# Split fp16 products for the projections of batches 2 to 7 in a gated cross-attention and mixture kernel

## The reference

```
xn = layernorm(x)
q = Wq xn + bq;  k = Wk ctx + bk;  v = Wv ctx + bv        (256x256 weights, 512 columns per batch)
q, k = rotary(q), rotary(k);  16 heads of 16 channels
x  = x + tanh(g0) * (Wm softmax(q k / 4) v + bm)
x  = x + tanh(g1) * moe(layernorm(x))                     (8 experts, top 2, 512 -> 1024 -> 512)
```

## Time and profile before

| | |
|---|---|
| median of 3 runs | 1136.09 us (1134.47 to 1137.49) |
| profiled execution | 1133.16 us |
| its span | 1131.3 us |
| TensorE matmul, weight load | 1079.3, 443.7 us busy |
| VectorE, ScalarE, GpSimd | 801.2, 684.7, 378.6 us busy |
| phases 3 to 12 | some 32 us each |

### The profile page before, as it was taken

One profiled execution on the slowest core, in us unless ns is written; L12 is line 12 of the kernel. 1 busy time (PEld: TensorE's weight loads), 2 busy tenths in 40 slices (PEclk: granted clock), 3 DMA queues, 4 the chain that ended last, 5 costly groups with the idle time before them and its releaser, 6 DMA issues.

```text
span 1131.3 us, 19036 instructions
## 1 busy us (share of the span) xinstructions
PE 1079.3 (95%) x5988; PEld 443.7 (39%) x5988; DVE 801.2 (71%) x1595; ACT 684.7 (61%) x934; POOL 378.6 (33%) x489
## 2 busy tenths in 40 slices
PE   8998999999999999988989999999999999999997
PEld 3322333333333333332344444444444444444443
DVE  7878898898988887888377575756547565755632
ACT  1277777777777777788765574646446464653421
POOL 3673636848483865532220011110111101111101
PEclk9999999999999999999989999999999999999999
DMA  6336435323234323202258685758657476883433
GB/s 199 117 94 210 163 107 197 110 94 107 78 114 132 104 79 104 92 31 88 80 215 265 138 222 102 203 118 223 141 111 198 119 218 141 203 170 59 70 61 47
DMA packets 182671, 150.60 MB, mean 133 GB/s; under 512 B 122672, under 2 KB 144176, under 8 KB 182576
## 3 DMA queue, kind: packets, MB, share of 16 engines
q1 hardware_dynamic: 171680, 128.91, 40.3%
q0 software_dynamic: 7456, 17.57, 7.9%
q10 hardware_dynamic: 3440, 2.94, 1.0%
HBM read 73.80 MB, written 41.23 MB: 102 GB/s over the span
## 4 chain that ended last, share of the span: by engine, by line
PE 77%; DVE 9%; ACT 7%; issue 4%; DMA 2%; SPq 1%; POOL 0%; POOLq 0%; DVEq 0%; ACTq 0%
PE psum L1291 36%; PE psum L1292 10%; PE psum L364 7%; PE psum L351 6%; PE psum L240 6%; ACT W L545 5%; DVE MX L737 4%; PE psum L339 3%; PE psum L289 3%; PE psum L256 2%; PE psum L381 2%; PE psum L271 1%; ACT W L495 1%; PE psum L308 1%; PE psum L277 1%
## 5 line engine op out<-in xcount | busy, mean ns | idle before, releaser
L545 ACT ACTIVATE W<-psum,es 128x512 f32<-128x512 f32 x512 | 321.4, 688 | 72.9 <-PE psum L351 71.6
L737 DVE TENSOR_REDUCE MX<-psum 128x2 f32<-128x1024 f32 x256 | 310.4, 1219 | 50.0 <-PE psum L339 47.6
L1291 PE MATMUL psum<-W,xT 128*128 128x512 f16 x1248 | 273.7, 379 | 0.0
L1291 PEld LDWEIGHTS psum<-W,xT 128*128 128x128 f16 x1248 | 121.5, 98 | 148.5 <-issue 2.9
L351 PE MATMUL psum<-stg 50*128 50x512 f16 x512 | 142.9, 386 | 21.6 <-ACT W L545 16.4
L1564 POOL DMA_INDIRECT out<-yb,target x34 | 53.1, 1562 | 291.5 <-ACT yb L1393 289.0
L1496 DVE TENSOR_TENSOR hh<-sg,psum 128x512 f32<-128x512 f32 x68 | 46.4, 685 | 145.0 <-ACT sg L1380 145.0
L1291 PE MATMUL psum<-W,hT 128*128 128x512 f16 x648 | 144.3, 379 | 0.0
L364 PE MATMUL psum<-W 128*32 128x512 f32 x1024 | 136.4, 605 | 0.0
L1380 ACT ACTIVATE sg<-psum,i 128x512 f32<-128x512 f32 x68 | 46.3, 681 | 143.3 <-PE psum L1291 120.6
L620 DVE SCALAR_TENSOR_TENSOR W<-stg,scw,W 128x1024 f16<-128x1024 f32 x96 | 117.3, 1279 | 11.7 <-ACT W L613 11.7
(11 more groups left out here) (241 smaller groups left out, 1359.3 us busy)
## 6 DMA issues: line engine op xcount, KB each, us to landing
stg<-in_w SPq DMA_DIRECT2D x16, 2048.0 KB, 8.9
stg<-in_wo SPq DMA_DIRECT2D x8, 2048.0 KB, 10.3
stg<-scr SPq DMA_DIRECT2D x183, 64.0 KB, 2.3
Xs<-zero SPq DMA_DIRECT2D x40, 264.0 KB, 3.2
scr<-W SPq DMA_DIRECT2D x32, 256.0 KB, 3.1
W<-W SPq DMA_DIRECT2D x60, 128.0 KB, 2.1
xs<-in_x SPq DMA_DIRECT2D x8, 512.0 KB, 4.3
out<-xs SPq DMA_DIRECT2D x8, 512.0 KB, 3.1
```

The costliest lines, as they stand in the source:

```text
L545: act.activation(m.Pb[:, c % 2, hh, :], m.psT[tile % 2], ACT.Exp, scale=m.es[:, hb // 2:hb // 2 + 1]).then_inc(S["exped"], 1)
L737: dve.tensor_reduce(m.MX[:, hb % 2, c0:c0 + 9:8], m.psS[tile % 2], AX_X, ALU.max, negate=True).then_inc(S["maxed"], 1)
L1291: return pe.matmul(out, rows, m.wh[(e % 2, w)][:, wp, cols], start=start, stop=stop)
```

## The change

For batches 2 to 7 the q, k and v projections use fp16 halves. A number a is scaled by a power of two and split in an upper half, fp16(a), and a lower half, fp16(a - upper). A product is upper*upper + upper*lower + lower*upper: three fp16 matmuls for one fp32 matmul. A q or k job has 6 matmuls of 512 columns, a v job 12 of 256. Batches 0 and 1 stay fp32.

- Weights: their largest values (one new reduction of Wv on VectorE in phase -1, one all-partition maximum on GpSimd at the end of phase -1), six small scale operations on VectorE (phase 0, slot 3), three upper halves on ScalarE (phase 0, slot 5), three lower halves on VectorE (phase 0, slots 8, 10, 12).
- Context of batch b: five more small operations in `k_scale` (odd phase, slot 4), the upper half on ScalarE (`ctx_upper`, odd phase, slot 6), the lower half on VectorE (`ctx_lower`, odd phase, slot 8).
- Rows: `norm` gets a factor 2^10 by one more small operation on GpSimd, the upper half is a copy on ScalarE (`x_upper`, even phase, slot 9), the lower half a subtraction on GpSimd (`x_lower`, even phase, behind the last scatter and ahead of `x1_root`). `xn` has one buffer for these batches.
- The emptying of q, k and v undoes the scales in its own scale operand.
- Start: `early(36)` becomes `early(20)`; ScalarE issues 3 of the 6 loads of the first q stack, SyncE the other 3; the second root stands ahead of ScalarE's share of the first k stack; `k_scale(1)`, the scaled bias and the copy of the number go from VectorE's prologue to phase -1 slot 3, phase 0 slot 6 and phase -1 slot 13.
- The load of the first expert's weights in phase 8 waits for one more batch's projections; loads of x and ctx share four semaphores each.

```diff
+        if b >= 2:
+            src = m.xh if w == 0 else m.ch[b]
+            if w == 0:
+                pe.wait_ge(S["halves_lower"], 1)
+                pe.wait_ge(S["x_lower"], b - 1)
+            else:
+                pe.wait_ge(S["halves_lower"], 2 + b)
+            for n, (it, wp, xp) in enumerate((it, *ps) for it in range(2) for ps in PARTS):
+                last = pe.matmul(bank, m.wqk[:, wp, w, it, t * 128:t * 128 + 128], src[:, xp, it, :], start=(n == 0), stop=(n == 5))
...
-            early(36)
+            early(20)
...
+    def weights_upper():
+        act.wait_ge(S["weights_known"], 3)
+        for w in range(3):
+            act.activation(m.wqk[:, 0, w] if w < 2 else m.wv[:, 0], m.wT[:, w], ACT.Copy, scale=m.sw[:, w:w + 1]).then_inc(S["halves_upper"], 1)
+    def ctx_upper(b):
+        act.wait_ge(S["k_scale"], b)
+        act.wait_ge(S[CTX_FREE[b][0]], CTX_FREE[b][1])
+        act.activation(m.ch[b][:, 0], m.cx[b], ACT.Copy, scale=m.scx[:, b:b + 1]).then_inc(S["halves_upper"], 1)
+    def x_upper(b):
+        act.wait_ge(S["xn"], 2 * b + 2)
+        act.wait_ge(S["projected"], 2 * (2 * b - 1) + 1)
+        act.copy(m.xh[:, 0], m.xn[:, 0]).then_inc(S["x_upper"], 1)
...
-    stack(act, m, S, 0, 0)
+    stack(act, m, S, 0, 0, (1,))
+    root(2, 2, 6)
     stack(act, m, S, 1, 0, (1,))
     job("k", 1)
-    root(2, 2, 6)
...
+        if b >= 2:
+            v = slice(b, b + 1)
+            step.more(last)
+            step(dve.tensor_scalar(m.pc[:, v], m.bigs[:, 6 + b:7 + b], 1e-30, None, ALU.max))
+            step(dve.tensor_scalar(m.pc[:, v].bitcast(I32), m.pc[:, v].bitcast(I32), 0x7F800000, None, ALU.bitwise_and))
+            step.more(dve.tensor_scalar(m.scx[:, v].bitcast(I32), m.pc[:, v].bitcast(I32), -1.0, float(268 << 23), ALU.mult, ALU.add))
+            step.more(dve.tensor_scalar(m.sk[:, v], m.pc[:, v], m.sc[:, 1 + b:2 + b], m.wfac[:, 1:2], ALU.mult, ALU.mult))
+            last = dve.tensor_scalar(m.sv[:, v], m.pc[:, v], m.wfac[:, 2:3], None, ALU.mult)
+            step.settle()
...
+    def weights_lower(w):
+        dve.wait_ge(S["halves_upper"], w + 1)
+        hi, lo = (m.wqk[:, j, w] if w < 2 else m.wv[:, j] for j in range(2))
+        dve.scalar_tensor_tensor(out=lo, in0=m.wT[:, w], scalar=m.sw[:, w:w + 1], in1=hi, op0=ALU.mult, op1=ALU.subtract).then_inc(S["halves_lower"], 1)
+    def ctx_lower(b):
+        dve.wait_ge(S["halves_upper"], 2 + b)
+        dve.scalar_tensor_tensor(out=m.ch[b][:, 1], in0=m.cx[b], scalar=m.scx[:, b:b + 1], in1=m.ch[b][:, 0],
+                                 op0=ALU.mult, op1=ALU.subtract).then_inc(S["halves_lower"], 1)
...
-            pool.wait_ge(S["projected"], 2 * (2 * b - 3) + 1)
+            if b == 2:
+                pool.wait_ge(S["projected"], 2 * 1 + 1)
+            else:
+                pool.wait_ge(S["x_lower"], b - 2)
+            step(pool.tensor_scalar(m.rstd[:, 2 * b:2 * b + 2], m.rstd[:, 2 * b:2 * b + 2], 2.0 ** 10, None, ALU.mult))
             norm(pool, m, S, b)
...
+        if ph % 2 == 0 and 2 <= b < NB:
+            pool.wait_ge(S["x_upper"], b - 1)
+            pool.tensor_tensor(m.xh[:, 1], m.xn[:, 0], m.xh[:, 0], ALU.subtract).then_inc(S["x_lower"], 1)
```

More of the change, by code:

```diff
@@ L251, in values @@
         b, half = i // 2, i % 2
-        pe.wait_ge(S[f"ctx{b}"], 16)
+        pe.wait_ge(S[f"ctx{b % 4}"], 16 * nth(b, 4))
         for cc in ccs:
             c = 2 * half + cc
+            if b >= 2:
+                pe.wait_ge(S["halves_lower"], 2 + b)
+                for n, (it, wp, xp) in enumerate((it, *ps) for it in range(2) for ps in PARTS):
+                    last = pe.matmul(m.psM[:, cc * 256:cc * 256 + 256], m.ch[b][:, xp, it, c * 128:c * 128 + 128], m.wv[:, wp, it, :],
+                                     start=(n == 0), stop=(n == 5))
+                continue
             for it in range(2):
@@ L494, in projected @@
         bank = m.psum[:, OWN[("k", 0)], :] if w and not hb else m.psM
-        empties(act.activation(m.qb[:, w, :], bank, ACT.Identity, bias=m.sbias[:, n, hb % 2:hb % 2 + 1], scale=m.sc[:, n:n + 1]), S, ("qk"[w], hb))
+        undo = m.sc[:, n:n + 1]
+        if hb >= 4:
+            act.wait_ge(S["weights_known"], 3)
+            undo = m.sk[:, hb // 2:hb // 2 + 1] if w else m.wfac[:, 0:1]
+        empties(act.activation(m.qb[:, w, :], bank, ACT.Identity, bias=m.sbias[:, n, hb % 2:hb % 2 + 1], scale=undo), S, ("qk"[w], hb))
     def flipped_back(hb):
@@ L524, in valued @@
             act.wait_ge(S["weighed"], 8 * (2 * b - 2))
[L525 removed]
+        to, bank = m.vT[:, b % 2, 2 * half:2 * half + 2, :, 0:16], m.psM.rearrange("p (c h d) -> p c h d", c=2, d=16)
+        if b >= 2:
+            act.wait_ge(S["k_scale"], b)
+            empties(act.activation(to, bank, ACT.Copy, scale=m.sv[:, b:b + 1]), S, ("v", i))
+        else:
+            empties(act.copy(to, bank), S, ("v", i))
+    def weights_upper():
+        act.wait_ge(S["weights_known"], 3)
+        for w in range(3):
+            act.activation(m.wqk[:, 0, w] if w < 2 else m.wv[:, 0], m.wT[:, w], ACT.Copy, scale=m.sw[:, w:w + 1]).then_inc(S["halves_upper"], 1)
+    def ctx_upper(b):
+        act.wait_ge(S["k_scale"], b)
+        act.wait_ge(S[CTX_FREE[b][0]], CTX_FREE[b][1])
[4 more added lines that the diff above has]
+        act.copy(m.xh[:, 0], m.xn[:, 0]).then_inc(S["x_upper"], 1)
     def rows_upper(b):
@@ L589, in scalar_attention @@
                 s = 2 * st + k
+                if ph == 0 and s == 5:
+                    weights_upper()
+                if ph % 2 and 2 <= (ph + 3) // 2 < NB and s == 6:
+                    ctx_upper((ph + 3) // 2)
+                if ph % 2 == 0 and 2 <= (ph + 4) // 2 < NB and s == 9:
+                    x_upper((ph + 4) // 2)
                 if ph % 2 and 0 <= (ph - 3) // 2 < NB and s == (13 if ph < LAST else 6):
@@ L885, in spread @@
     def spread(ph, s):
+        if ph == -1 and s == 3:
+            k_scale(1)
+        if ph == -1 and s == 10:
+            dve.tensor_reduce(m.bigv[:, 0:1], m.wT[:, 2, :, :].rearrange("p i o -> p (i o)"), AX_X, ALU.max, apply_absolute_value=True).then_inc(S["weights_known"], 1)
+        if ph == 0 and s == 3:
+            weight_scales()
+        if ph == 0 and s in (8, 10, 12):
+            weights_lower((s - 8) // 2)
+        if ph % 2 and 2 <= (ph + 3) // 2 < NB and s == 8:
+            ctx_lower((ph + 3) // 2)
+        if ph == -1 and s == 13:
+            dve.wait_ge(S["router"], 16 * 7)
+            dve.tensor_copy(m.zero[:, NUMBER:NUMBER + 1].bitcast(I32), m.tok[:, 16:17]).then_inc(S["zeroed"], 1)
+        if ph == 0 and s == 6:
+            dve.wait_ge(S["small"], 64)
+            dve.wait_ge(S["tg"], 2)
+            dve.tensor_scalar(m.tbm[:, :], m.bm[:, :], m.tg[:, 0:1], None, ALU.mult).then_inc(S["tbm"], 1)
         b = (ph + 4) // 2
@@ L976, in vector_attention @@
     variances(2, 6)
-    k_scale(1)
     dve.wait_ge(S["std"], 2)
@@ L1159, in sync_attention @@
     keep(1, 0)
+    stack(sp, m, S, 0, 0, (0,))
     stack(sp, m, S, 1, 0, (0,))
```

50 lines of the change are left out of this document (36 added, 14 removed).

## The result

The changed kernel took 1150.14 us (median of 4 executions, 1148.68 to 1154.86), the kernel before 1135.55 us in the same comparison: ratio 1.0137, 95% interval 1.0117 to 1.0157. The forecast was 1141.5 us, between 1131 and 1150. So the kernel got slower, as forecast, but the loss, 14.6 us, is nearly three times the 5.4 that were forecast.

The account below looks back on a forecast made before the run. VectorE was taken to limit q to k, mostly TensorE k to q, with GpSimd's run holding back q. Periods +4.9 and start +0.7, rounded down to +5.4, gave 1138.6 us as profiled, 1141.5 as median; range 1131 to 1150.

Parts of the forecast that it names:

- I take +0.7, between 0 and 3.5: Start up to phase 0: earlier TensorE start offset by work moved to phase -1, new scale and half work; net +0.7 us.
- q to k, forecast: First piece, odd phase's q job to its k job: new VectorE work of 2.3 us, net mostly +1.75 us.
- k to q, forecast: Second piece, k job to next odd q: cheaper jobs save 1.9 us, but GpSimd's lower half lets q gain less.
- Jobs of 1.40 us: Split q, k and v jobs on TensorE take 1.40 us instead of 1.93, saving 0.53 each over 36 jobs.
- Rival 3: Weight loads not hidden at 256 columns: v takes 2.57 us, q and k up to 1.99; total 1150; chance 0.08.
- GpSimd's run binds: Second piece: lower half of rows behind the last scatter holds back q; TensorE idle 0.5 to 1.3 us, phases 5 to 11.
- Rival 1: GpSimd doesn't bind: the rows' lower half ends before TensorE wants q; total 1135; chance 0.22.
- VectorE limits the first piece: From q to k VectorE is the limit, so its 2.3 us of new work lengthen the piece, near 21.5 instead of 19.9.
- Rival 2: Faster: VectorE's 2.3 us fill waits, GpSimd doesn't bind; first piece grows by less than 0.9 us; total 1127; chance 0.17.
- x1_apply: VectorE waits 0.4 us at this step in the first piece, because x1_root stands behind GpSimd's subtraction.
- Rival 4: A larger stall, of ScalarE's upper half or VectorE's small operations behind GpSimd, 1 us more per period; total 1147; chance 0.08.

Follow-up runs that it names:

- the version with early reductions: The changed kernel with VectorE's maximum of Wv and GpSimd's all-partition maximum moved to the prologue; median of all 18 executions 1137.8 us.
- first run: First measurement of the version with early reductions: 1137.09 us (10 executions), ratio 1.0028 to the kernel before.
- second run: Later measurement of the version with early reductions, same program: 1140.82 us (8 executions), ratio 1.0053 to the kernel before.
- the version with both edits: The version with early reductions, plus GpSimd's lower half of rows ahead of its k rotary and the context's lower half moved there from VectorE; 1145.35 us, ratio 1.009.

## Why the prediction was wrong in size

**The step that failed** is the one on the start: "I take +0.7, between 0 and 3.5". The list of the change had the all-partition maximum on GpSimd at the end of phase -1, and the sum gave VectorE's and ScalarE's work there a price and this one none. The start measured +8.8 us at the q job of phase 1, though TensorE began phase -1 at 31.08, 3.6 us sooner and not 1.8. Alone in the kernel before the operation costs 7 to 9 us, an ordinary small operation in its place 1.1 at most, and with it in the prologue the changed kernel takes 1137.8 in place of 1150.1 us. Part of these prices is waiting and part the lower clock behind the waits. The profile of before had most of the price to show: GpSimd's timeline at the end of phase 13 has

```profile
480.89 0.38 POOL L626 PARTITION_ALL_REDUCE mxa<-mxr  x1 [5.82 <-issue]
```

and the groups by line give this operation, 24 times 0.353 us, 11.7 us of idle time of the same kind, in two places. That is the idle time ahead of it; the 9 us behind it can't be read there, since GpSimd's next operation waits for ScalarE. The sum took neither.

**The rest of the sum** can be held against the version with early reductions, which has everything else of the change. By the two ratios it is 3 to 6 us slower than the kernel before; 5.4 were forecast. That the sum agrees is luck in part: up to the q job of phase 11 its periods cost 2.3 us in one run and 4.6 in the other, where 5.3 were forecast, and its start -0.4 and +5.8, where 0.7 was. Its parts, from the windows (us, difference to before; phases 1, 3, 5, 7, 9, 11):

```
q to k, forecast            +1.75 +1.75 +2.15 +1.7  +2.15 +1.5
q to k, first run           +0.7  +1.3  +2.8  +1.2  +0.8  +0.9
q to k, second run          +0.4  +1.4  +2.8  +1.0  +1.4  +0.9
q to k, changed kernel      +2.4  +1.2  +1.3  +3.1  +1.1  +1.4
k to q, forecast            -2.1  +0.15 -0.6  -0.65 -1.0
k to q, first run           -2.2   0.0  -0.6  -0.6  -1.1
k to q, second run          -2.2  +1.3  -0.6  -0.7  -0.3
k to q, changed kernel      -1.0  -0.3  +1.5  +0.1  -1.0
```

- Jobs of 1.40 us: 1.40 to 1.47 measured at full clock. Rival 3, unhidden weight loads, is out, for 256 columns too: 12 matmuls with 12 weight tiles in 1.43 us, each load 98 ns. The Trainium skill (TensorE: Matmul & The Clock Gate, The mechanism), by which a load overlaps matmuls only with another row group, is not borne out here either.
- GpSimd's run binds: right for phases 5 to 9. q waited for it 1.88 us in phase 5 and 0.98 in phase 9, and 1.89, 0.95 and 0.93 in phases 5, 7 and 9 of the first run with early reductions; "0.5 to 1.3" had been forecast. In phase 11, named in the forecast too, q waited for VectorE. The second pieces of the version with early reductions follow the forecast to 0.15 us in one run. Rival 1 is out.
- VectorE limits the first piece: right, and somewhat too dear. 1.3 us per piece on the mean, with the q job's 0.53 in it, against 1.8; phase 5's +2.8 contains a clock of 0.93. Rival 2 wanted under +0.9 and is out by the mean, though single pieces (0.7 and 0.8 in the first run) are that short.
- x1_apply: 0.4 us of wait had been forecast; in the changed kernel it waited nowhere, in the version with both edits 0.79, 0.26 and 0.25 us in phases 5, 7 and 9. This term was wrong in place. Rival 4's mechanism, VectorE's small operations behind GpSimd, is there in the kernel before already; the change adds 4.3 us of it to VectorE between the q job of phase 1 and the k job of phase 11, 2.7 of them in L855 of phase 7. What that costs in time was not separated.
- Not forecast at all: the granted clock, which stands behind 17.8 us of longer busy time between two executions of the same matmuls. All pieces of the earlier trace rows have 1.00, and I took that for a property of the code. It falls to 0.50 for some 4 us behind a stall of 3.75 us, and to 0.68 in the 4 us around one of 1.89 us (below). Where the changed kernel's periods cost 8.3 us and those of the version with early reductions 2.3 and 4.6, most of the difference stands in windows at 0.89 to 0.97.

**What stays open.** When the clock falls isn't shown: behind the wait of 1.89 us of q of phase 5 it fell in both runs with early reductions, and behind the same wait of 1.88 us in the changed kernel it stayed at 1.00. So why the changed kernel has more such stretches in phases 5 to 10 than the first run with early reductions, with nearly the same work and waits, I can't say; a kernel that fills the stalls with other matmuls was not tried, since no accumulator bank is free at those places. Why GpSimd is idle around the all-partition maximum the profile doesn't show either; only that it is, whether or not anything waits.

## What to carry to other kernels

When a change adds an operation of a kind that is rare on its engine, read the idle time in brackets on both sides of its siblings in the trace of before, and not only its length; put it beside its siblings, where it cost 0.64 us here. Before moving work into an engine's idle time, ask what that idle time waits for: work placed behind the same transfer is as late as the transfer, and that depends on what stands ahead of it in the issuing queue. Let the range for a new stall of TensorE reach above its length, since the clock behind it can be lower: 7.3 us of delay became 13.1 in the run with the all-partition maximum alone, 4.1 us of it as the same matmuls at a lower clock.

## What the runs showed of the hardware

- An all-partition maximum on GpSimd between ordinary operations: 0.38 us of work, 6.1 us idle before it and 9.1 to 9.2 us behind it, in two kernels; 0 with a `tensor_scalar` in its place; 0.24 before and 0.64 of its own beside other all-partition operations.
- Granted clock 0.50 for 4 us directly behind a stretch in which TensorE worked 1.13 of 4 us, and at times a drop behind shorter waits too (not behind the 1.88 us at 224.69 in the changed kernel). The windows around q of phase 5, which waits 1.89 us for GpSimd at 212.87, in the first run with early reductions:

```profile
208.00:212.00 4.00, 2.99 (x20) 1.01 (x20) 3.86 (x7) 3.12 (x6) 3.61 (x4) 1.00 0.49 154
212.00:216.00 4.00, 3.13 (x14) 0.77 (x14) 2.04 (x4) 0.88 (x2) 3.00 (x13) 0.68 0.49 147
216.00:220.00 4.00, 3.65 (x27) 1.25 (x29) 3.80 (x7) 3.53 (x7) 3.79 (x3) 0.89 0.36 115
```

- A VectorE operation on 128 x 2 elements that took 2.91 us (0.17 for its neighbour) and ended with GpSimd's 2.14 us subtraction; 18 such operations of 0.6 to 1.34 us in the kernel before, all ending with one of GpSimd.
- SyncE's queue: six transfers of zeros took 4.95 us to issue and twelve reads 7.07, and the swap behind them was issued 11.0 us after the q job, in place of 6.4 without the zeros and the load ahead of it.
- Twelve fp16 matmuls of 256 columns, each with its own 128 x 128 weights, in 1.43 us on the chain.
